# Folding pooled rows on TensorE with the roles of weights and stream exchanged: four batches in four column tiles, then a copy and four transposes

## What is computed

```python
topi, topv = top_k(softmax(logits, over the tokens), K=8)      # for each image and expert
gathered = take_along_axis(x, flat_idx)                        # (16, 8, 64, 128) rows
pooled = einsum('bked,bke->bed', gathered, topv)               # sum of 8 rows by weight
h = gelu([pooled, 1] @ weight1[e]);  out = [h, 1] @ weight2[e]
outputs = zeros.at[b, flat_idx].add(einsum('beo,bke->bkeo', out, topv))
x = t + outputs
```

## Time and profile before

| what | value |
|---|---|
| time, median of 3 runs | 2157.56 us (2151.57 to 2160.16) |
| time of the profiled execution | 2155.56 us |
| its span, first to last instruction | 2153.8 us |
| mean granted TensorE clock | 0.957 |
| busy: PE, DVE, ACT, POOL | 1873.0, 1822.8, 1882.0, 1939.2 us |
| the tail, from the first pooling matmul to the end of the span | 1959.37 to 2153.8 us |

### The profile page before, as it was taken

One profiled execution on the slowest core, in us unless ns is written; L12 is line 12 of the kernel. 1 busy time (PEld: TensorE's weight loads), 2 busy tenths in 40 slices (PEclk: granted clock), 3 DMA queues, 4 the chain that ended last, 5 costly groups with the idle time before them and its releaser, 6 DMA issues.

```text
span 2153.8 us, 42420 instructions
## 1 busy us (share of the span) xinstructions
PE 1873.0 (87%) x11917; PEld 1286.6 (60%) x11917; DVE 1822.8 (85%) x4612; ACT 1882.0 (87%) x5020; POOL 1939.2 (90%) x2068
## 2 busy tenths in 40 slices
PE   6999999999999999999999999999999987636991
PEld 6866666666666666666666666666666643213570
DVE  4689999999999898989899999999999899624670
ACT  6899999999999999999999999999999987743420
POOL 5799999999999999999999999999999999961387
PEclk9999999999999999999999999999999998765995
DMA  5498888887888888888788888888788676694963
GB/s 188 157 262 222 228 223 206 226 229 216 218 218 235 224 227 210 224 231 222 215 216 231 229 224 220 212 229 227 213 222 223 178 182 162 165 263 124 282 104 32
DMA packets 111068, 447.92 MB, mean 208 GB/s; under 512 B 10575, under 2 KB 52404, under 8 KB 61684
## 3 DMA queue, kind: packets, MB, share of 16 engines
q1 hardware_dynamic: 81140, 302.61, 42.9%
q0 software_dynamic: 29696, 142.61, 34.2%
HBM read 306.78 MB, written 138.41 MB: 207 GB/s over the span
## 4 chain that ended last, share of the span: by engine, by line
ACT 38%; POOL 21%; issue 17%; PE 16%; DVE 5%; ACTq 1%; DMA 1%; POOLq 0%; SPq 0%; DVEq 0%
ACT U L553 16%; POOL U L430 8%; POOL U L435 7%; ACT zT L516 6%; ACT UT L510 6%; PE G L747 4%; ACT LTS L580 3%; ACT LTS L525 3%; PE T L729 3%; PE O L680 2%; POOL zn L451 2%; POOL out_dram L490 2%; PE T L736 1%; ACT zn L574 1%; POOL U L442 1%
## 5 line engine op out<-in xcount | busy, mean ns | idle before, releaser
L553 ACT ACTIVATE U<-xa,nA,rA 128x128 f32<-128x128 f32 x1948 | 803.7, 483 | 2.1 <-issue 1.3
L747 PEld LDWEIGHTS G<-UT 128*128 128x128 f32 x4096 | 536.8, 192 | 226.5 <-issue 225.3
L430 POOL TENSOR_TENSOR U<-U,bet 128x512 f32<-128x512 f32 x512 | 651.4, 1272 | 2.2
L435 POOL TENSOR_TENSOR U<-U,rO 128x512 f32<-128x512 f32 x512 | 532.2, 1040 | 20.3 <-ACT rO L533 19.3
L747 PE MATMUL G<-UT 128*128 128x128 f32 x4096 | 542.0, 275 | 0.0
L680 PE MATMUL O<-U,MT 128*128 128x512 f32 x1024 | 529.5, 599 | 3.0 <-DVE U L938 3.0
L451 POOL TENSOR_TENSOR zn<-U,rZ 128x512 f32<-128x512 f32 x414 | 446.6, 1079 | 11.0 <-ACT rZ L564 10.3
L936 DVE BATCH_NORM_STATS2 stO<-O 128x6 f32<-128x256 f32 x1024 | 386.8, 423 | 50.2 <-PE O L680 49.5
L729 PE MATMUL T<-ident,U 128*128 128x128 f32 x2048 | 324.3, 281 | 119.1 <-ACT UT L510 108.6
L729 PEld LDWEIGHTS T<-ident,U 128*128 128x128 f32 x2048 | 224.6, 142 | 318.1 <-issue 314.1
L954 DVE BATCH_NORM_STATS2 stA<-xa 128x6 f32<-128x256 f32 x1024 | 386.8, 426 | 31.8 <-DMA xa<-in_x 28.5
(11 more groups left out here) (151 smaller groups left out, 1655.0 us busy)
## 6 DMA issues: line engine op xcount, KB each, us to landing
xa<-in_x SPq DMA_DIRECT2D x128, 1024.0 KB, 6.3
U<-in_x POOLq DMA_DIRECT2D x128, 1024.0 KB, 10.8
out_dram<-U SPq DMA_DIRECT2D x128, 1024.0 KB, 8.6
U<-in_L_ffn_weight SPq DMA_DIRECT2D x112, 256.0 KB
LTS<-in_L_ffn_weight SPq DMA_DIRECT2D x16, 256.0 KB
xa<-out_dram,UT POOLq DMA_INDIRECT x64
out_dram<-U,UT POOLq DMA_INDIRECT x64
zT<-in_L_ffn_weight SPq DMA_DIRECT2D x1, 128.0 KB
```

The lines of the kernel that those rows point to most:

```text
L430: gp.tensor_tensor(rows(a, i), rows(a, i), bet_b, ALU.add).then_inc(S["gb"], 1)
L435: gp.tensor_tensor(rows(a, i), rows(a, i), rO[:, i // 2 % 2, i % 2 * TI:(i % 2 + 1) * TI].unsqueeze(2).to_broadcast([P, TI, W]), ALU.mult) ...
L553: last = sc.activation(utile(a, i, j), xa[:, k % XR, h * W:(h + 1) * W], ACT.Identity, scale=rA[:, k % 2, h:h + 1], bias=nA[:, k % 2, h:h ...
L747: last = te.matmul(G[:, 0:P], v, v, start=(i == 0 and j == 0), stop=(i == NI - 1 and j == TI - 1))
```

## The change

PE's roles are exchanged: `FW` (16 columns) is loaded as weights and `R` (128 columns) is streamed. Image `n` goes to column tile `n % 4` and to the 128-column block `n // 4` of `T0`, so the result has experts on the partitions (16 of each 32) and channels in the columns. A new ACT copy `raw(q)` brings the whole bank to `PR` in SBUF, `turn0(q)` transposes its four 128 x 128 blocks back into `T0`, and `pooled(q)` copies from there, skipping the 16 unused columns of each 32. Both halves of `pooling(q)` now stand where only the first stood.

```diff
+        PR = over(half, 4 * P, at=at_h)
...
+            def raw(q):
+                act.wait_ge(R_["pmm"], 2 * q + 2)
+                sc.activation(PR, T0[:, :], ACT.Copy).then_inc(R_["raw"], 1)
+
             def pooled(q):
-                act.wait_ge(R_["pmm"], 2 * q + 2)
+                act.wait_ge(R_["trp"], q + 1)
 
                 wait(act, R_["h"], 4 * (q - 1))
                 sc.activation(PT[:, q % 2, :, :].rearrange("p e n -> p n e"),
-                              T0[:, 0:NB * EQN].rearrange("p (n e) -> p n e", e=EQN), ACT.Copy).then_inc(R_["p_done"], 1)
+                              T0[:, :].rearrange("p (n e) -> p n e", e=32)[:, :, 0:EQN], ACT.Copy).then_inc(R_["p_done"], 1)
...
             for t in range(SLOTS):
+                if t == 0:
+                    raw(0)
                 if t < NG and t % 4 == 0:
                     pooled(t // 4)
...
                     sc.activation(C[:, u % 4, :], MB[:, :], ACT.Copy).then_inc(R_["c"], 1)
+                if t % 4 == 3 and t // 4 + 1 < Q:
+                    raw(t // 4 + 1)
...
-            def pooling(q, h):
-
-                if h == 0:
-                    wait(pe, R_["p_done"], q)
-                pe.wait_ge(R_["fw"], 2 * q + h + 1)
-                for n in range(8 * h, 8 * h + 8):
-                    last = te.matmul(T0[:, n * EQN:(n + 1) * EQN], R[:, q, n, :], FW[:, q % 2, n, :], start=True, stop=True)
-                last.then_inc(R_["pmm"], 1)
+            def pooling(q):
+
+                wait(pe, R_["p_done"], q)
+                for h in range(2):
+                    pe.wait_ge(R_["fw"], 2 * q + h + 1)
+                    for n in range(8 * h, 8 * h + 8):
+                        i, c = n % 4, n // 4
+                        last = te.matmul(T0[32 * i:32 * i + EQN, c * W:(c + 1) * W], FW[:, q % 2, n, :], R[:, q, n, :],
+                                         start=True, stop=True)
+                    last.then_inc(R_["pmm"], 1)
+
+            def turn0(q):
+                pe.wait_ge(R_["raw"], q + 1)
+                for c in range(4):
+                    last = te.transpose(T0[:, c * P:(c + 1) * P], PR[:, c * P:(c + 1) * P], ident[:, :])
+                last.then_inc(R_["trp"], 1)
...
             for t in range(SLOTS):
                 if t == 0:
-                    pooling(0, 0)
+                    pooling(0)
                 if t < NG and t % 4 == 0:
-                    pooling(t // 4, 1)
+                    turn0(t // 4)
                 if t < NG:
                     layer1(t)
                 if t % 4 == 3 and t // 4 + 1 < Q:
-                    pooling(t // 4 + 1, 0)
+                    pooling(t // 4 + 1)
```

More of the change, by code:

```diff
@@ L212, in program @@
         s_w = [sem(f"s_w{i}") for i in range(WR // 4)]
-        tnames = ("sel part cut code rowf idx codt codc row eq fst nf idxs rbn rvar rln rr wv cen fw pmm p_done "
+        tnames = ("raw trp sel part cut code rowf idx codt codc row eq fst nf idxs rbn rvar rln rr wv cen fw pmm p_done "
                   "h ge trh ht o ou tro ott xt v cmm c").split()
```

## The result

The changed kernel takes 2169.84 us (median of 12 executions, 2161.97 to 2173.63) against 2158.86 us for the kernel before (12, 2151.57 to 2164.97): ratio 1.0044, 95% interval 1.0028 to 1.006, some 10 us slower. The prediction had said +2 us with a range up to 2167. The profiled execution takes 2165.97 us, its span is 2164.1 us.

The account below looks back on a forecast made before the run. POOL's indirect DMAs were taken to bound the tail; order alone gave +0.9 us, with clock losses +3.2, so +2 was taken: 2157.6 for the profiled execution, 2159.5 for the median, range 2153 to 2167.

Parts of the forecast that it names:

- POOL as the bound, unit 3 and unit 5 as the two points: Tail: POOL's indirect DMAs set the end, which moves by the larger of unit 3's shift and unit 5's less 2.1 us.
- the slack of 2.1 us: Tail, POOL's unit 5: it could start at 2062.35 and starts at 2064.48, so a delay up to 2.1 us is free.
- quarter 1: Slot 3: whole pooling waits for the second FW, but the old second half's 3.60 us pay for it; about 0.
- The price of the new matmuls: Pooling: a half costs 0.55 us at the high clock or 0.95 at the low one, like line 804.
- The rival in which the tiles don't run side by side: Pooling: a half takes 2.2 us or more instead of 0.55, four times on the path; about 2164; chance 7%.
- Quarter 0: Start of the tail, low clock: cheaper matmuls after the second FW bring layer1 earlier, -1.3 us.
- The cost of the order: Slots 7 and 11: work once hidden under the wait for the second FW queues behind it; +2.2 and +2.0 us.
- The clock, the step that failed: Slots 7 and 11: low clock after each stall costs 1.2 us, half of a 5 us stretch's 2.5; nothing for slot 3.
- the longest rival: Slots 7 to 15: the clock stays low throughout and PE replaces POOL as the bound; +13 us, 2170; chance 4%.
- slower beyond doubt: Slots 7 to 15: clock stays low, slots take 11.9 us, PE bounds, 4.3 us a slot; +13, 2170; chance 4%.
- the clock falls for longer: Tail: slot 1's clock rise comes later and each stall costs the full 2.5 us; about +7, 2164.5; chance 20%.
- The rule for weight loads: Pooling: the skill page's rule that loads overlap only across row groups, 1.07 us a half instead of 0.55; cited, not adopted.

Follow-up runs that it names:

- a3_fill: Changed kernel plus ten additional full-width matmuls per later quarter between its two pooling halves, order and waits untouched; ratio 1.0006 to the kernel before.
- c4: The changed kernel run again, on the chip of the b and c sets; 2152.64 us, ratio 1.0052 to the kernel before.
- b1: a1_split, but with quarter 2's pooling left whole in slot 7 as in the changed kernel; 2143.74 us, ratio 0.9997 to the kernel before.
- a2_wait_only: Kernel before with one edit: pooling's first half in slots 3, 7 and 11 also waits for the second FW; ratio 1.0124 to the kernel before.
- a4_late: Changed kernel with later quarters' second pooling half between layer2 and combine in slots 3, 7, 11, and raw ahead of copy C; ratio 0.9973 to the kernel before.
- b4_late_old: Kernel before, old matmul form, with later quarters' second pooling half between layer2 and combine in slots 3, 7, 11; ratio 1.0026 to the kernel before.
- set a: First of three sets of experiments, on one chip, ratios taken to the kernel before run beside them; that kernel's median there was 2158.03 us.
- a1_split: Changed kernel with both halves of each later quarter's pooling put back where the kernel before has them; 2155.51 us, ratio 0.9987 to the kernel before.
- c1_wait_fill: a2_wait_only plus twelve additional full-width matmuls ahead of its wait in slots 3, 7 and 11; 2144.64 us, ratio 1.0035 to the kernel before.
- b3_place_only: Kernel before, old matmul form, with both halves of later quarters' pooling in slots 3, 7 and 11; no raw, no turn0; ratio 1.0074 to the kernel before.

## Why the prediction was wrong

It was wrong in its size and its range: +2 us forecast, up to 2167 allowed, about +10 measured (2169.84). The sign of the largest term, its place and its mechanism were named; its size was missed. Point by point:

- **POOL as the bound, unit 3 and unit 5 as the two points.** Right. Up to unit 3 the tail shifted by 0.5 us (+0.9 to +2.1 forecast), the loss is at units 4 to 6, and in a3_fill, the changed kernel with its clock kept, slot 11 is 2.0 us longer and POOL then waits 0.53 us ahead of unit 5: the slack of 2.1 us is just used up. The parts up to unit 3 came out less exactly than their sum: quarter 1 gave 0.8 us (0 forecast; turn0 ran at the high clock there, 0.66 us for the 1.0 worked out), and POOL's unit 0 came 0.35 us later in the tail, not about 2.
- **The price of the new matmuls.** Right: a half takes 0.62 us at the high clock and 1.06 at the low one by its records (0.55 and 0.95 forecast), as line 804's form says. The rival in which the tiles don't run side by side is out. `raw` and `pooled` take 0.60 us each, `turn0` 0.66 and 1.11.
- **Quarter 0.** -1.3 forecast. From the second `FW` (1961.07 + 0.29 = 1961.36) to layer1 (1964.99) are 3.6 us; before they were 4.7: -1.1.
- **The cost of the order.** +2.2 for slot 7 and +2.0 for slot 11 forecast. a3_fill has +2.5 and +2.0. The changed kernel's PE stalls 3.02 and 2.58 us there (some 3 forecast).
- **The clock, the step that failed.** "A stretch of 5 us wholly at the low level loses up to 2.5 us. I take half of that, 1.2 us, for each of the slots 7 and 11." For slot 7 the term came out, 14.89 - 13.61 = 1.3 us, but by chance: with the same stall the slot took 13.31 us in c4 and 17.21 in b1. Behind the stall of slot 11 it failed. Against a3_fill, slot 11 loses 16.62 - 12.88 = 3.7 us, slot 12 12.24 - 6.63 = 5.6 and slot 13 8.26 - 6.62 = 1.6, together 11 where 1.2 stood. The low level was taken to last half of one stretch of 5 us; it lasted through most of 25 us, and PE was busy in the last 15 of them without a gap, so I was also wrong to think that work would bring the clock back at once. The trace of before had two counterexamples. In its first 15 us of tail, show PE busy from 1959.37 on with one gap of 0.69 us and still at the low level at 1974.43; I used this for a rival alone, and not for the term. And behind the wait of slot 3 the low level lasts some 14 us, of which the earlier trace rows show only the first stretch:

```profile
1990.00:1995.00 5.00, 4.31 (x21) 0.50 0.90 281
1995.00:2000.00 5.00, 4.98 (x61) 0.60 0.36 119
...
2025.00:2030.00 5.00, 5.00 (x67) 0.87 0.92 191
```

The last line also corrects what was said against the longest rival: the 0.79 of 2020 to 2025 isn't a clock that came back within the stretch; the clock fell in it and came back in the next one.

- **The rival "slower beyond doubt".** It had the mechanism and the price per slot: a slot of 11.9 us (12.24 measured) in place of 6.6, PE in POOL's place, "it decides from three such slots". One such slot came in full and two in part (11 and 13), and the loss was some 10 us. It was given 4%, and no case stood between one stretch of low clock and nine slots of it. The rival "the clock falls for longer", at +7 and 20%, still counted 2.5 us a stall.
- **The rule for weight loads.** What was cited from the Trainium skill, "TensorE: Matmul & The Clock Gate", Part 3, that a weight load overlaps only across row groups, would have made a half 1.07 us at the high clock; 0.62 was measured. What the Trainium skill says on the same page under "HAM oscillation", that waits between bursts bring the engine back to half rate, is borne out by a2_wait_only (granted 0.50 behind the wait of 3.55 us) and a3_fill (granted 1.00 behind slot 11 with the stall filled); but not each wait did it, as the 1.51 us in a4_late show. The page's lesson was in the prediction's text and not in its sum.

## What to carry to other kernels

In this kernel a wait of some 3 us on TensorE was not priced by its length. Price such a wait with the slots behind it at the low clock, as many as the trace shows such a stretch to last elsewhere, and ask if PE then becomes the bound. When pieces of work are joined in program order, look for the wait that the second piece brings with it and what is queued behind that wait; here putting the second half behind layer2, where PE comes to it 5.6 us after the first half instead of 3.6 and doesn't wait, turned a loss of 10 us into a gain of 4 to 6.

## What the runs showed of the hardware that was not expected

- The low clock can outlast the wait ahead of it by far: over 30 us after a wait of 3.55 us in a2_wait_only, with PE busy 5.00 us of nearly every 5. That makes one edited line, which waits in three slots, cost 26 us, 1.2% of the time.
- It isn't the same in every execution of a kernel: the changed kernel ranges over 11 us in each of its two sets, and its time goes with the mean granted clock of the execution (correlation -0.82 and -0.83; -0.92 in b4_late_old). This isn't so for each kernel: in set a it is 0.06 for a1_split and 0.22 for the kernel before, which still range over 5 and 11 us. What decides it is open.
- The clock also fell behind the old matmul form (128 columns loaded, 16 streamed) with a wait of 0.59 us only, in c1_wait_fill, and with 1.14 to 1.58 us in b3_place_only and b4_late_old, and it did so in none of the profiled executions of the new form in a4_late's order in slots 7 to 13, which have waits of up to 1.51 us there. Whether the form of the matmuls does this, or what stands around them, was not tried by itself and stays open. So the length of the wait alone doesn't tell whether the clock falls.
